# A window-attention kernel whose TensorE round is put in another order: all 64-row tiles in a row, then the 128-row ones

## What is computed

```python
x = x + zca(group_norm(x), weight, bias)            # whitening of 16 groups of 4 channels
x = x + window_attention(group_norm(x))

# window_attention, on windows of 7x7 = 49 tokens:
xn   = (x - bn_mean) * inv + bn_beta
tok  = windows of xn, (16*8*8, 49, 64)
qk   = (tok @ qk_w.T).reshape(-1, 49, 2, 16, 16)   # 16 heads of 16, so four windows of tokens in one
q, k = qk[:, :, 0], qk[:, :, 1]
attn = softmax(einsum('bhqd,bhkd->bhqk', q, k) * scale)
v    = relu(tok @ v_w.T)
out  = einsum('bhqk,bhkd->bhqd', attn, v)
```

## Time and profile before

| | us |
|---|---|
| median of 3 runs (lowest, highest) | 534.57 (533.85, 535.39) |
| the profiled execution | 536.41 |
| its span | 534.7 |
| PE busy in it | 455.6 (85%) |
| DVE busy | 343.5 (64%) |
| ACT busy | 293.0 (55%) |
| POOL busy | 192.7 (36%) |

### The profile page before, as it was taken

One profiled execution on the slowest core, in us unless ns is written; L12 is line 12 of the kernel. 1 busy time (PEld: TensorE's weight loads), 2 busy tenths in 40 slices (PEclk: granted clock), 3 DMA queues, 4 the chain that ended last, 5 costly groups with the idle time before them and its releaser, 6 DMA issues.

```text
span 534.7 us, 40426 instructions
## 1 busy us (share of the span) xinstructions
PE 455.6 (85%) x18274; PEld 358.6 (67%) x18274; DVE 343.5 (64%) x1079; ACT 293.0 (55%) x514; POOL 192.7 (36%) x159
## 2 busy tenths in 40 slices
PE   7579981498577799999999999999999999999972
PEld 6357761432265587778777787777877787777861
DVE  4523337868345577777777777777777777777662
ACT  1112220046474477677676676676776776776730
POOL 8300000000213245455455454454454454554522
PEclk9679995679979999999999999999999999999998
DMA  8960000000111142432414224142341424324132
GB/s 311 420 242 4 5 4 0 1 1 0 46 57 65 56 120 85 128 115 91 124 68 141 90 102 141 61 134 85 112 136 76 120 83 128 113 94 125 68 87 61
DMA packets 30645, 52.18 MB, mean 98 GB/s; under 512 B 5248, under 2 KB 20096, under 8 KB 29696
## 3 DMA queue, kind: packets, MB, share of 16 engines
q1 hardware_dynamic: 30592, 51.50, 28.4%
HBM read 12.95 MB, written 12.85 MB: 48 GB/s over the span
## 4 chain that ended last, share of the span: by engine, by line
PE 80%; DVE 8%; issue 7%; POOL 1%; ACT 1%; DMA 0%; SPq 0%; POOLq 0%; DVEq 0%; ACTq 0%
PE ps L868 17%; PE ps L812 11%; PE ps L904 10%; PE ps L890 10%; PE ps L828 7%; PE ps L843 6%; PE ps L723 6%; PE ps L782 5%; PE ps L735 4%; PE ps L875 4%; DVE dupm L413 1%; DVE X L583 1%; DVE rmax L660 1%; PE ps L757 1%; DVE yz L551 1%
## 5 line engine op out<-in xcount | busy, mean ns | idle before, releaser
L303 POOL TENSOR_TENSOR X<-X,otok 128x392 f32<-128x392 f32 x64 | 109.2, 1706 | 202.5 <-DVE otok L693 202.5
L660 DVE TENSOR_REDUCE rmax<-ps 113x16 bf16<-113x784 f32 x128 | 120.7, 943 | 44.4 <-PE ps L843 44.4
L868 PE MATMUL ps<-diag,qk_all 64*49 64x98 f32 x4096 | 131.6, 245 | 6.8 <-issue 6.3
L868 PEld LDWEIGHTS ps<-diag,qk_all 64*49 64x49 f32 x4096 | 112.4, 121 | 27.8 <-issue 19.0
L350 ACT ACTIVATE prob<-ps 113x784 f32<-113x784 f32 x128 | 105.6, 825 | 44.3 <-PE ps L875 43.1
L297 POOL TENSOR_SCALAR xs<-X,affined 128x392 f32<-128x392 f32 x64 | 69.1, 1080 | 131.8 <-DVE affined L651 118.4
L875 PE MATMUL ps<-mdiag,sel 64*49 64x98 bf16 x2048 | 113.2, 203 | 2.7 <-issue 2.7
L365 ACT ACTIVATE vst<-ps 49x256 f32<-49x256 f32 x256 | 96.7, 378 | 6.6 <-PE ps L828 3.2
L357 ACT ACTIVATE qk_all<-ps 128x784 f32<-128x784 f32 x64 | 52.7, 824 | 75.6 <-PE ps L812 75.6
L812 PE MATMUL ps<-xs,wqk 64*64 64x392 f32 x512 | 57.6, 517 | 16.8 <-issue 10.1
L677 DVE RECIPROCAL rden<-ps 128x98 f32<-128x98 f32 x64 | 49.4, 771 | 33.6 <-PE ps L890 33.6
(11 more groups left out here) (162 smaller groups left out, 407.0 us busy)
## 6 DMA issues: line engine op xcount, KB each, us to landing
diag<-qk_all SPq DMA_DIRECT2D x256, 98.0 KB, 2.0
out<-X SPq DMA_DIRECT2D x32, 392.0 KB, 4.2
X<-x_in SPq DMA_DIRECT2D x7, 1024.0 KB, 14.6
X<-x_in SPq DMA_DIRECT2D x7, 544.0 KB, 15.5
X<-x_in SPq DMA_DIRECT2D x4, 256.0 KB, 3.6
X<-x_in SPq DMA_DIRECT2D x2, 192.0 KB, 4.6
X<-x_in SPq DMA_DIRECT2D x1, 160.0 KB, 4.6
wqk<-w_qk SPq DMA_DIRECT2D x1, 64.0 KB, 18.0
```

The source lines that it names most:

```text
L303: g.tensor_tensor(rows_of(u), rows_of(u), otok[u % 2][:].rearrange("p k a s -> p k s a"), ALU.add).then_inc(S["x_ready"], 1)
L660: v.tensor_reduce(rmax[u % 3][0:ROW, :, 8 * k:8 * k + 8], ps[0:ROW, B_S:B_S + 2, 0:8 * POS].rearrange("p h (v q) -> p h v q", q=POS), AX.X ...
L868: mm(ps[64 * e:64 * e + POS, B_ST + hh, col:col + 2 * POS], qk[u % 3][r, g, k, 2 + x_, :], diag[u % 3][r, e::2, g, k, x_, :], start=True, ...
```

## The change

On PE the pieces of a round stand in another order. Before: project_qk(w), exp(u,0), max(s,0), project_v(s), sum_weights(z), max(s,1), exp(u,1), weigh_values(z), turn_max(s). After: project_qk(w), max(s,0), exp(u,0), project_v(s), max(s,1), exp(u,1), turn_max(s), sum_weights(z), weigh_values(z). So a round changes between 64-row and 128-row tiles twice, not four times.

On DVE, `divide` of a unit goes to the head of the next round, ahead of both maxima, and `invert` goes behind the second maximum and `spread_max`. On POOL `add` is one round later. The turned maxima lie in bank `B_O`, not in `B_S`. Of PE's waits those are left out that another wait implies once the order is the new one, and the wait for `mdiag` stands ahead of `weigh_values`. Per round in the loop there were 11 waits and there are 8.

```diff
-            for i in range(-3, UNITS + 1):
+            for i in range(-3, UNITS + 2):
                 if has(i + 3):
                     normalise(i + 3)
-                if has(i - 1):
-                    add(i - 1)
+                if has(i - 2):
+                    add(i - 2)
...
-                                ps[:, B_S, MT:MT + POS].rearrange("p (o q) -> p o q", o=1).broadcast_to([P, 2, POS]),
+                                ps[:, B_O, MT:MT + POS].rearrange("p (o q) -> p o q", o=1).broadcast_to([P, 2, POS]),
...
             def project_qk(u, at):
                 need("xs_ready", at)
-                need("v_ready", at)
+                need("prob1", at)
...
             def scores_for_exp(u, k, at):
-                need(("prob1", "prob0")[k], at)
+                if k == 1:
+                    need("prob0", at)
+                elif u >= UNITS - 2:
+                    need("prob1", at)
...
-                        if k == 0 and g == 0 and x_ == 0:
+                        if u < 2 and k == 0 and g == 0 and x_ == 0:
                             need("mdiag_ready", at)
...
             def sum_weights(u, at):
-                need("rden_ready", at)
+                if u >= UNITS - 2:
+                    need("rden_ready", at)
...
-            def weigh_values(u, at):
-                need("o_ready", at)
+            def weigh_values(u, at, later):
+                if u < UNITS - 2:
+                    need("mdiag_ready", later)
+                else:
+                    need("o_ready", at)
```

More of the change, by code:

```diff
@@ L697, in _ @@
             dve.wait_ge(S["zeros_ready"], 3)
-            for i in range(-1, UNITS + 1):
+            for i in range(-1, UNITS + 2):
                 s, z = i + 1, i - 1
+                if has(z - 1):
+                    divide(z - 1)
                 if has(s):
                     maximum(s, 0)
-                if has(z):
-                    invert(z)
-                if has(s):
                     maximum(s, 1)
@@ L707, in _ @@
                 if has(z):
+                    invert(z)
                     broadcast(z)
-                    divide(z)
         @block.tensor
@@ L805, in project_qk @@
                 need("xs_ready", at)
-                need("v_ready", at)
+                need("prob1", at)
                 if u == 1:
                     pe.wait_ge(S["qk_ready"], 1)
+                if u == 2:
+                    pe.wait_ge(S["v_ready"], 1 + CREDIT["v_ready"])
                 for o in range(2):
@@ L854, in turn_max @@
                         q = 2 * hh + x_
-                        ins = mm(ps[32 * q:32 * q + 32, B_S, MT:MT + POS], rmax[u % 3][0:ROW, hh, :],
+                        ins = mm(ps[32 * q:32 * q + 32, B_O, MT:MT + POS], rmax[u % 3][0:ROW, hh, :],
                                  identb[0:ROW, 64 * x_:64 * x_ + POS], start=True, stop=True)
@@ L912, in _, with body @@
             pe.wait_ge(S["mix_dve"], MIX)
-            def body(i, at, landed):
+            def body(i, at, later, landed):
                 u, s, w, z = i, i + 1, i + 2, i - 1
@@ L917, in body @@
                     project_qk(w, at)
+                if has(s):
+                    scores_for_max(s, 0, at, landed)
                 if has(u):
@@ L920, in body @@
                 if has(s):
-                    scores_for_max(s, 0, at, landed)
                     project_v(s, at)
-                if has(z):
-                    sum_weights(z, at)
-                if has(s):
                     scores_for_max(s, 1, at, landed)
@@ L928, in body @@
                     scores_for_exp(u, 1, at)
-                if has(z):
-                    weigh_values(z, at)
                 if has(s):
                     turn_max(s, at)
+                if has(z):
+                    sum_weights(z, at)
+                    weigh_values(z, at, later)
             def plain(i):
-                body(i, i + 3, 64 * ((i + 1) // 3 + 1))
+                body(i, i + 3, i + 4, 64 * ((i + 1) // 3 + 1))
             for i in range(-2, 2):
@@ L941, in _ @@
                 for r in range(3):
-                    body(2 + r, pe.snap(3 * q + 5 + r), landed)
+                    body(2 + r, pe.snap(3 * q + 5 + r), pe.snap(3 * q + 6 + r), landed)
             for i in range(62, UNITS + 1):
```

## The result

| | before | after |
|---|---|---|
| median, us (lowest, highest) | 534.98 (533.85, 535.88) | 545.29 (544.52, 546.01) |
| span of the profiled execution | 534.7 | 543.1 |

The ratio of after to before is 1.0194, with a 95% interval of 1.0167 to 1.0220: the change makes the kernel slower by 10.3 us. Forecast were 543.7.

The account below looks back on a forecast made before the run. Bound: a dependence chain through DVE's queue, 5.81 us a round against PE's 5.54. A pass of 3 x 5.81 + 0.05 = 17.48 for 17.00, over 19 passes, gives +9.1 us: 543.7; 8 in 10 within 534 to 551.

Parts of the forecast that it names:

- The ring: Dependence chain from turned maxima through denominators, DVE's reciprocal, shuffles, division and both maxima back again: 5.81 us a round.
- PE's own path: PE's round from one projection L812 to the next, without waits for DVE's maxima: 5.54 us, the same as before.
- the stall on the exponential: On PE before exp(u,1), waiting for ACT's exponential of half 0: a new stall of 0.3 us, exp(u,1) starting at 2.94.
- PE's waits: PE would wait 0.3 us for `max0` and again for `max1` in a round.
- rounds of about 5.8 us with hardly a difference for the jump: Sign to look for in the changed kernel's profile, where the jump is the loop's jump back.
- The jump of the loop: Between weighted values and L812, costing 0.36 us; with 0.24 of slack, 0.12 is left, 0.05 taken per pass.
- The waits left out: PE's register waits, 11 to 8 a round: hidden where matmuls are queued; the end of a round taken as 0.18 us.
- The changes of tile: Drains on PE before 128-row tiles, 0.10 after values and 0.11 after denominators: 0.21 us a round removed.
- Clock and DMAs: Granted clock stays at 1.00; DMAs into `diag` land at about 6.23, read at 6.49, hidden by 0.26 at least.
- PE's path as the bound: Rival: PE sets the round, not DVE's queue; not slower, 534.6 us, 530.6 to 543.7; chance 0.15.
- The drains won in full: Rival: all tile-change losses on PE are saved, 57 x 0.21 = 12 us, giving 522.6 us; chance 0.06.
- The longer ring: Rival: PE's restart from idle and DVE beside POOL's add add 0.15 a round: 5.96, 551.3 us; chance 0.17.

## Why the prediction was right, step by step

- *The ring*, forecast 5.81, measured 5.82. It sets two turns of three; in the third PE's own path does, by 0.10. Step by step, forecast and measured: maxima to denominators 0.03 and 0.04; to the reciprocal 0.96 and 0.93; to the shuffles 0.86 and 0.81; to the division 0.89 and 0.90; to the first maximum 0.49 and 0.48; to PE 1.06 and 1.11; to the second maximum 0.40 and 0.43; to the turned maxima 1.12 and 1.12. Four of the eight terms (the prediction speaks of ten) were off by 0.03 to 0.05, two each way: a reciprocal's result reaches the shuffle in 0.04, not 0.09, and the first maximum takes 0.96 behind the division, not the 0.91 that it takes behind the reciprocal. The mechanism was right, but that the sum came out within 0.01 is luck: the errors cancel.
- *PE's own path*, forecast 5.54 and 5.9 with the jump. The kernel with the division moved shows it: 5.48, 5.49 and 5.94 as medians of the three rounds. The end of a round was 0.10 (353.47 + 0.72 to 354.29), not 0.18; the stall on the exponential was there as forecast, with exp(u,1) at 340.70 - 337.75 = 2.95 for 2.94. That the second maximum ties with it, 0.03 us apart, the prediction had not seen.
- *PE's waits*, forecast 0.3 for `max0` and again for `max1`. In the round shown the second scores come 0.36 late and the turned maxima 0.33 (they follow exp(u,1) by 1.34, for 1.01 where PE doesn't wait). In the round behind the jump there is neither, and the projection starts 5.48, 5.83 and 6.25 apart: the sign "rounds of about 5.8 us with hardly a difference for the jump" is there in the turned maxima (5.82, 5.82, 5.92), not in the projection, which isn't part of the ring.
- *The jump of the loop.* Of 0.36, I had found 0.12 left over and then taken 0.05. A pass is 17.57 - 3 x 5.82 = 0.11 longer than the ring: the full 0.12 was right, and the 0.05 a shortening without a row behind it. This and the 0.01 in the ring are the 0.09 a pass, 1.7 us over 19 passes, by which 543.7 fell short.
- *The waits left out* were priced at nothing in the ring, since I looked at where they had stood, in a full queue. In the new order `rden_ready` would have stood between the turned maxima and the denominators, inside the ring, at 0.1 us, and `v_ready` ahead of the projection at as much. The sum wasn't touched, as the change does leave it out, but the expectation for the run with the waits back failed by this.
- *The changes of tile*, forecast at 0.21 us a round, measured 0.27 in their own place and 0.24 in another. The loss was real and still no guide to the time.
- *Clock and DMAs.* The granted clock from 200 to 500 us was 1.00 before and after, and PE never waited for `diag` between 200 and 500 us, nor for POOL.
- *The rivals.* PE's path as the bound is what the moved division gives, 535 us. The drains won in full never come, not even without the ring. The longer ring would have had to be 5.96 and was 5.82; PE's restart showed no extra, and nothing of DVE's in the ring was held by POOL's add.

## What to carry to other kernels

When a piece is moved on one engine, follow what depends on it once round all engines until you come back to the piece itself, and add up the starts: such a ring is a lower bound for the round, and busy shares, here 65% on the engine that held it, do not show it. Here it was shortened by taking an instruction out of it into a place where its engine waits anyway, one instruction further on. Once it is gone the next chain decides: here two of them lay within 0.03 us of each other, so that shortening one gave 0.02 us a round and shortening both 0.28. An explicit wait cost between nothing and 0.1 us in this kernel, by its place and not by its kind, so price it at the place to which it moves, and first of all where that lies inside a ring.

## What was not expected of the hardware

An operation of DVE with two SBUF operands (128 x 98 f32, 0.25 us) took 1.08 us when POOL's add was running and ended 0.10 us behind it; a copy from SBUF to SBUF (0.22 us) took 1.05 and ended 0.08 behind it. With one operand from PSUM the product kept its 0.25 us in the middle of the same add. The Trainium skill, SBUF — State Buffer, section Terms, describes a pair of ports for which DVE and GpSimd arbitrate, held for a whole instruction while the loser blocks fully. The trace agrees in that the delay lasted until POOL's instruction had ended. That the PSUM operand is what frees DVE of it is shown by the pair of runs for these two products only; for the copy no such pair was run.
